# Two 3x3 convolutions of a Trainium2 kernel as 64x32 instead of 32x32 products, with shifted strips copied inside SBUF

## What is computed

```python
x = x + _L0_conv_ref(_gn(x), w_real, w_imag, b_real, b_imag)  # rfftn, complex 3x3 conv, irfftn
x = x + _L1_conv_ref(_gn(x))                                  # gates per row of one channel against another
x = x + _L2_conv_ref(_gn(x), L2_conv_W)                       # 3x3 convolution, 16 -> 16 channels, padding 1
x = x + _L3_conv_ref(_gn(x), L3_conv_weight)                  # the same, other weights
```

## Time and profile before

| | |
|---|---|
| runs | 4795.12, 4809.72, 4811.2 us, median 4809.72 |
| profiled execution | span 4801.7 us from its first to its last instruction; no time of its own beside the span is recorded, the median lies 8.0 us above it |
| busy | PE 95%, PEld 61%, DVE 61%, ACT 52%, POOL 0% |
| mean granted TensorE clock | 0.968 of full speed |
| DMA | 468 MB, 97 GB/s over the span |

### The profile page before, as it was taken

The page is one execution under the profiler, slowest core; times in us unless marked ns, Lnnn a source line. Parts: engine busy times, 40 slices in busy tenths (PEclk is TensorE's granted clock), DMA queues, the critical chain, the costliest instruction groups (busy, mean ns, idle before and its releaser), DMA issues.

```text
span 4801.7 us, 221653 instructions
## 1 busy us (share of the span) xinstructions
PE 4548.2 (95%) x84784; PEld 2936.4 (61%) x84784; DVE 2925.9 (61%) x10604; ACT 2487.6 (52%) x7085; POOL 3.2 (0%) x14
## 2 busy tenths in 40 slices
PE   4999999999999999999999999999999999998889
PEld 1555675556655566556665556655666557655566
DVE  1777717766277662777527765377744777257770
ACT  4455355544555445554455544555445554544435
POOL 0000000000000000000000000000000000000000
PEclk8999999999999899999999989999899999999999
DMA  7443015630166202662036510366004650034304
GB/s 196 111 124 100 4 29 172 176 102 4 47 177 176 79 3 61 178 177 63 4 86 177 176 41 3 105 176 174 24 3 120 177 163 19 3 111 122 90 4 143
DMA packets 290069, 468.11 MB, mean 97 GB/s; under 512 B 25392, under 2 KB 92144, under 8 KB 289264
## 3 DMA queue, kind: packets, MB, share of 16 engines
q1 hardware_dynamic: 289392, 458.29, 33.1%
HBM read 323.98 MB, written 134.22 MB: 95 GB/s over the span
## 4 chain that ended last, share of the span: by engine, by line
PE 91%; DVE 3%; issue 3%; DMA 1%; SPq 1%; ACT 1%; ACTq 0%; DVEq 0%
PE ps L1247 35%; PE ps L1165 19%; PE ps L1150 18%; PE ps L1158 6%; PE ps L1174 5%; PE ps L1024 5%; DMA x<-x 1%; PE ps L1273 1%; PE ps L1070 1%; PE ps L1071 0%; PE ps L1097 0%; PE ps L1305 0%; PE ps L1219 0%; SPq L360 0%; PE ps L1112 0%
## 5 line engine op out<-in xcount | busy, mean ns | idle before, releaser
L1247 PE MATMUL ps<-x,conv_s 32*32 32x512 f32 x49104 | 1728.0, 603 | 20.8 <-DVE x L948 16.7
L1247 PEld LDWEIGHTS ps<-x,conv_s 32*32 32x32 f32 x49104 | 1252.8, 103 | 437.9 <-issue 196.1
L563 ACT ACTIVATE x<-ps,vec 128x256 f32 (+1 forms) x1024 | 492.0, 495 | 1003.1 <-PE ps L1165 1003.1
L1165 PE MATMUL ps<-hil,shared 128*128 128x256 f32 x4096 | 993.6, 386 | 0.0
L814 DVE COPY vsb<-ps 128x512 f32<-128x512 f32 x512 | 329.9, 686 | 1043.6 <-PE ps L1150 1043.6
L1165 PEld LDWEIGHTS ps<-hil,shared 128*128 128x128 f32 x4096 | 740.2, 190 | 273.8 <-issue 194.1
L802 DVE SCALAR_TENSOR_TENSOR shared<-xin,trig 128x256 f32<-128x256 f32 x2048 | 821.6, 441 | 57.3
L629 ACT ACTIVATE x<-ps,vec 64x512 f32<-64x512 f32 (+1 forms) x768 | 527.2, 686 | 395.9 <-PE ps L1247 385.6
L1150 PE MATMUL ps<-shared 32*32 32x512 f32 x16384 | 656.4, 605 | 0.0
L620 ACT ACTIVATE x<-ps,vec 128x512 f32 x512 | 347.9, 685 | 439.6 <-PE ps L1247 439.6
L1150 PEld LDWEIGHTS ps<-shared 32*32 32x32 f32 x16384 | 306.2, 104 | 280.0 <-issue 216.8
(11 more groups left out here) (170 smaller groups left out, 2720.6 us busy)
## 6 DMA issues: line engine op xcount, KB each, us to landing
xin<-x SPq DMA_DIRECT2D x512, 256.0 KB
out<-x SPq DMA_DIRECT2D x512, 256.0 KB
shared<-x SPq DMA_DIRECT2D x448, 256.0 KB, 5.0
shared<-t_strip SPq DMA_DIRECT2D x512, 96.0 KB, 3.6
x<-x SPq DMA_DIRECT2D x64, 256.0 KB, 8.1
x<-t_proj SPq DMA_DIRECT2D x1, 2048.0 KB, 11.8
hil<-t_hil SPq DMA_DIRECT2D x1, 560.0 KB, 12.1
trig<-t_trig SPq DMA_DIRECT2D x1, 512.0 KB, 11.8
```

Of the source, the lines that this page charges most:

```text
L563: ins = nc.scalar.activation(split_in(strip_of(s))[:, q, :], split_in(ps[:, bank, :])[:, q, :], ACT.Identity, bias=v1(MEAN), accum_out=sum ...
L1165: mm = pe.matmul(split_in(ps[:, BY + 2 * odd + e, :])[:, int(q < 2), :], xt[:, e, q, :], hil[:, q, 0:HALF], start=False, stop=True, skip_g ...
L1247: mm = pe.matmul(ps[TM * cg:TM * cg + TM, banks[k], :], conv_s[TM * rg:TM * rg + TM, kw, second, :], x1[TM * rg:TM * rg + TM, of, kw:kw + ...
```

## The change

- **64x32 products.** Each output quarter is now made by one product per tap, with 64 partitions of input (two quarters, half the array's rows) and 64x32 weights: 8 products a tap and pair, 24 a pair instead of 48, on 8 tiles of 64x32. `halved`, LAG2 and LAG3 go. The order over a pair is tile by tile with the two strips in turn; each of the 8 tiles is used once per tap. `conv_s` keeps its size; its 64-row blocks have two kinds.
- **Shifted strips.** The two quarters that an output needs lie in one half of the partitions for half of the outputs only. For the others a second copy of the strips, with the quarters moved, is kept in `ring`: up to 12 strips in layer 2 (3 groups of 2 pairs, RING2) and 8 in layer 3 (2 groups, RING3). It is filled by DMA from `x1` (SBUF to SBUF). Layer 2: per group of two pairs 6 DMAs on SP, two of 32 partitions x 4 strips and four of 32 x 2; the first two pairs apart, three of their DMAs each on SP and three on ScalarE's queue, after `keep_zh`. Layer 3: 2 DMAs per group, 96 x 4 strips and 32 x 4. Either way 1 MiB a group. A group's copy waits for gates (layer 2), for the last eviction of layer 2 (layer 3), and for the group that last used its slots: three groups back in layer 2, two groups back in layer 3.
- **Squares** of layer 2: ScalarE squares the even strip of a pair after evicting it, VectorE the odd one; `red` and its copy go. GATES_AHEAD is 16, before it was 12.
- **Memory.** `ring` lies over `planes`, `wst` and part of `strip`, so the first `make_planes` of the next image waits until all but two pairs of layer 3 are done, those of strips 2 and 3 until all are, and four table loads move to after group 2 of layer 3.
- Stores of the last image go out two groups behind in layer 3. The bias of layer 3 takes 12 products (24 records), before 24 (L1305, 48 records). The pads of `ring` are set by one more operation on POOL and one on DVE.

```diff
-DEPTH2, LAG2 = 4, TAPS + 1
-DEPTH3, LAG3 = 3, TAPS
+DEPTH2, DEPTH3 = 4, 3
+BLOCKS = 4
+RING2, RING3 = 3, 2
+COPIES2, COPIES3 = 6, 2
+CONV_FREE = 3
...
-GATES_AHEAD = 3 * GROUP
+GATES_AHEAD = 4 * GROUP
...
+            def copy2(i):
+
+                for n in range(2):
+                    sp.wait_ge(gated, i * STRIPS + 2 * n + 3)
+                    sp.sem_inc(s_sp, 1)
+                    for to, of in blocks2(PAIRS - 1 - n, 1, slot2(n))[0::2]:
+                        sp.dma_start(to, of).then_inc((copied0, copied2[0])[n], 16)
+                for g in range(1, PAIRS // 2):
+                    sp.wait_ge(gated, i * STRIPS + min(STRIPS, BLOCKS * g + BLOCKS + 1))
...
+                        sp.wait_ge(convolved, cv(i, 1 + 2 * (g - RING2) + 2))
...
+                    for to, of in blocks2(PAIRS - 2 - 2 * g, 2, slot2(2 * g + 1)):
+                        sp.dma_start(to, of).then_inc(copied2[g % RING2], 16)
+
+            def copy3(i, g):
+
+                if g == 0:
+                    sp.wait_ge(evicted, ev(i, 1 + STRIPS))
+                    sp.sem_inc(s_sp, 1)
+                if g >= RING3:
+                    sp.wait_ge(convolved, cv(i, 1 + PAIRS + 2 * (g - RING3) + 2))
...
+                sp.dma_start(ring[0:P - TM, slot:slot + BLOCKS, 1:1 + N], x1[TM:P, s:s + BLOCKS, 1:1 + N]).then_inc(copied3[g % RING3], 16)
+                sp.dma_start(ring[q3, slot:slot + BLOCKS, 1:1 + N], x1[q0, s + 1:s + 1 + BLOCKS, 1:1 + N]).then_inc(copied3[g % RING3], 16)
...
-                act.wait_ge(convolved, i * CONVOLVED + 1)
+                for n in range(2):
+                    act.wait_ge(gated, i * STRIPS + 2 * n + 3)
+                    act.sem_inc(s_act, 1)
+                    for to, of in blocks2(PAIRS - 1 - n, 1, slot2(n))[1::2]:
+                        act.dma_start(to, of).then_inc((copied0, copied2[0])[n], 16)
+                act.wait_ge(convolved, cv(i, 1))
...
+                    nc.scalar.activation(junk, strip_of(STRIPS - 2 - n * 2), ACT.Square,
+                                         accum_out=cols[:, 3, bass.ds(STRIPS - 2 - n * 2, 1)]).then_inc(a_c_squared, 1)
...
+                dve.wait_ge(convolved, cv(i, -2))
+                dve.sem_inc(s_dve, 1)
                 for k in range(2):
                     make_planes(steps_of(k), k, k, u0 + 1, 0)
+                dve.wait_ge(convolved, cv(i, 0))
...
+                def products(banks, outputs, strips, kw):
+
+                    for j in range(TILES):
+                        for k in range(2):
+                            cg, h, slot, kind = outputs(strips[k])[j]
+                            rows = slice(HP * h, HP * h + HP)
+                            of = x1[rows, strips[k], kw:kw + N] if slot is None else ring[rows, slot, kw:kw + N]
+                            mm = pe.matmul(ps[TM * cg:TM * cg + TM, banks[k], :], conv_s[rows, kw, kind, :], of,
+                                           start=(kw == 0), stop=(kw == TAPS - 1), skip_group_check=True)
+                    return mm
```

More of the change, by code:

```diff
@@ L53 @@
 AXB, AXC, AXS = 0, 1, 2
+CONV_BLOCKS = ((0, 0, 0), (1, 0, 1), (2, 0, 0), (3, 0, 1), (1, 1, 0), (3, 1, 1))
 ZR = 96
@@ L112, in tables @@
     eye_conv = np.zeros((P, 2, TAPS, 2, TM))
-    for rg in range(TILES):
+    for rg, kind, second in CONV_BLOCKS:
         for c in range(C):
-            eye_conv[TM * rg + C + c, :, 1, 0, c] = 1.0
-            eye_conv[TM * rg + c, :, 1, 1, C + c] = 1.0
+            if second:
+                eye_conv[TM * rg + c, :, 1, kind, C + c] = 1.0
+            else:
+                eye_conv[TM * rg + C + c, :, 1, kind, c] = 1.0
     zsel = np.zeros((ZR, P + ZR))
@@ L162, in placed @@
         for kw in range(TAPS):
-            for second in range(2):
+            for rg, kind, second in CONV_BLOCKS:
                 for r in range(2):
@@ L350, in ev, with cv, slot2, blocks2 @@
             return i * EVICTED + n + EVICT_FREE
+        def cv(i, n):
+            return i * CONVOLVED + n + CONV_FREE
+        q0, q1, q2, q3 = (slice(TM * k, TM * k + TM) for k in range(TILES))
+        def slot2(n):
+            return BLOCKS * (n // 2 % RING2) + 2 * (1 - n % 2)
+        def blocks2(first, pairs, slot):
+            low = first * 2
+            across = lambda of, s, to: (ring[to, slot:slot + 2 * pairs, 1:1 + N], x1[of, s:s + 2 * pairs, 1:1 + N])
+            second = lambda of, s, to, k: (ring[to, slot + k:slot + 2 * pairs:2, 1:1 + N], x1[of, s:s + 2 * pairs:2, 1:1 + N])
+            above = across(q1, low - 1, q2) if low else (ring[q2, slot + 1:slot + 2 * pairs, 1:1 + N], x1[q1, 0:2 * pairs - 1, 1:1 + N])
+            return (above, across(q3, low, q0), second(q0, low, q3, 0), second(q2, low, q3, 1), second(q2, low + 1, q1, 0), second(q0, low + 1, q1, 1))
         @block.sync
@@ L442, in image @@
                     for pair in range(2):
-                        load_pair(i + 1, pair, 2 * pair)
-                for n in range(PAIRS):
-                    if more and n >= PAIRS - (STRIPS - DEFERRED):
-                        sp.wait_ge(evicted, ev(i, 1 + STRIPS + 2 * n + 2))
-                        sp.sem_inc(s_sp, 1)
-                        store(i, n - (PAIRS - (STRIPS - DEFERRED)))
-                    elif not more:
-                        for e in range(2):
-                            store(i, 2 * n + e)
+                        for e in range(2):
+                            load_x(i + 1, pair * 2 + e, pair, 2 * pair + e)
+                copy2(i)
+                for g in range(PAIRS // 2):
+                    copy3(i, g)
+                    if more and g == RING3:
+                        for pair in range(2):
+                            load_tables(i + 1, pair, 2 * pair)
+                    for e in range(BLOCKS if not more else 2):
+                        if not more and g >= RING3:
+                            store(i, BLOCKS * (g - RING3) + e)
+                        elif more and g >= PAIRS // 2 - (STRIPS - DEFERRED) // 2:
+                            store(i, 2 * (g - PAIRS // 2 + (STRIPS - DEFERRED) // 2) + e)
+                if not more:
+                    for s in range(STRIPS - BLOCKS * RING3, STRIPS):
+                        store(i, s)
             image(0, True, False)
```

165 lines of the change are left out of this document (83 added, 82 removed).

## The result

Before, the runs gave a median of 4810.5 us (4795.1 to 4811.7, 4 runs), after it 4670.8 us (4660.4 to 4680.2, 4 runs): a ratio of 0.9714, 95% interval 0.9690 to 0.9737. The change makes the kernel 139.6 us faster. The forecast was 4525, a gain of 286. The median lies inside the forecast's range of 4455 to 4720, but only about half of the gain came (49%).

What follows compares the result with a forecast made beforehand. TensorE bounds the kernel, by something in feeding 16 tiles. Gains of 138 (layer 2), 133 (layer 3), 8 (last image), 9 (bias), less 2, make 286 us: 4801.7 to 4516 span, 4524 with 8 added; forecast 4525, range 4455 to 4720.

Steps and rivals of the forecast that it cites:

- Part 1, the streaming: Layer 2's products: rounds of 0.43 us on 8 tiles, a pair 2.56 us instead of 3.10, gaining 16.2 us an image.
- rival 2: Streaming in layers 2 and 3 gains nothing, as the loss belongs to four tiles per row group; 4795 us, chance 0.1.
- Part 2, the start: Start of layer 2: 4 us lost waiting for first copies, 5 us gained by the second pair, net +1 an image.
- Part 3, layer 3: Layer 3 falls from 120.2 to 99.1 us; 19 us taken as gained in each of seven images, 133 in all.
- T: Time of a group's copies in layer 3, 6.0 us; what exceeds one group of 5.12 us is waited for.
- the term of 2.4 us: Part of the layer 3 copies' time that isn't data: fastest 256 KB landing of 3.3 us, of which 0.9 is data.
- that base: Layer 3 with no copy ever waited for: 95.6 us, from stream, slow start and column work.
- Rival 1: Copies over 32 or 96 partitions run slower than loads: 4565 us at 4.8 us per MiB, 4685 at 5.8; 4600-4780, chance 0.2.
- The last image: Its layer 3: copies plus stores, 7.2 us a group, leave 109.8 us as it is, 90 at full overlap; 8 us taken.
- Small parts: Bias halved gains 8.6 us in all, sharing squares 0 after the last pair, late `make_planes` loses 2.
- If both squares had stayed on DVE: Layer 2: DVE's work of 2.7 us would have capped each pair, against 2.06 with one square moved to ACT.
- Rival 3: Copies at half the loads' rate, 146 GB/s, 7.2 us per MiB, make the kernel slower: 4945 us, chance 0.08.

Runs made afterwards that it cites:

- 5: Also wide3: changed kernel, layer 3's copies from the second group on over 128 partitions x 2 strips, straight, same bytes; 4636.0 us.
- 6: Also straight3: changed kernel, layer 3's copies from the second group on keep 96 and 32 partitions but stay in their own rows; 4689.5 us.
- 3: Also nostore: changed kernel with 56 of the last image's 64 stores left out, copies kept; 4618.3 us.
- 4: Changed kernel with the last image's layer 3 copies of 32 partitions issued on ScalarE's queue, stores staying on SP's; 4690.1 us.
- 2: Changed kernel with layer 3's copies made pair by pair, in half as large pieces and four slots of two strips; 4605.3 us.
- 10: Also dvesq: changed kernel with both squares of layer 2 on VectorE again; 4675.8 us.
- twoact: Changed kernel with the 32-partition copy issued on ScalarE's queue from layer 3's third group on, beside SP's of 96; 4699.4 us.

## Why the prediction was half right

**Part 1, the streaming: right.** 2.575 us a pair instead of 2.56, and the weight loads (timeline, start of layer 3) come 8 at a time, 0.43 us apart:

```profile
1705.86 0.12 PEld L1332 LDWEIGHTS ps<-x,conv_s 64*32 64x32 f32 x4 [0.30 <-issue]
1705.87 0.12 PEld L1332 LDWEIGHTS ps<-shared,conv_s 64*32 64x32 f32 x4
...
1706.29 0.12 PEld L1332 LDWEIGHTS ps<-x,conv_s 64*32 64x32 f32 x4 [0.30 <-issue]
```

Four tiles share each half of the rows and a round still takes 1024 columns at 2.4 GHz, so rival 2 fell. The loads of both halves come while products of both halves are in flight, and nothing of the 0.43 us is lost to them. The Trainium skill, "TensorE: Matmul & The Clock Gate", Part 3, says that weight loads overlap products only when the row group differs; this trace does not agree with it. What costs 16 tiles 0.09 us a round is still open: no run took it apart.

**Part 2, the start: right in the loss, and in the gain by luck.** The start of layer 2, third image (gate, first copies, tail product):

```profile
1596.29 0.74 DVE L1035 TENSOR_SCALAR x<-x,cols,gate_b  x2 [0.24 <-issue]
...
1598.94 4.41 SPq L447 DMA_DIRECT2D shared<-x  x6
1598.94 4.13 ACTq L690 DMA_DIRECT2D shared<-x  x6
...
1603.65 1.03 PE L1357 MATMUL ps<-x,conv_s 64*32 64x512 f32 x1 [5.67 <-DMA shared<-x]
```

TensorE starts 7.4 us after the first gate, against 3.2 in the earlier trace rows: 4.1 us later, forecast 4. The second pair is evicted 10.9 us after the start instead of the 13.4 forecast. The bias takes 0.88 us instead of 2.16. Layer 2 with the bias was forecast at 138 + 8.6 us and brought 143.6. Two errors cancel in that. The third image, from which the 19.2 us before were read, is not typical: its first 10 us of layer 2 ran at a granted clock of 0.50, and so two others, while in five images the second pair was evicted 13.1 to 14.8 us after the start. The mean is 16.0 before and 10.3 after, so the gain was 5.6 us a start, against 5 forecast. No copy of layer 2 was late, at a DMA share of 0.78 (forecast 0.7).

**Part 3, layer 3: this is the step that failed.** Its value for the copies' time, T = 2.4 + 3.6 = 6.0 us, was too small, and so were the 3.5 us of waiting that followed from it; and it put what the clock loses after a wait at nothing. The landing of L469 (768 KB) and, on the lines of the copies, L470's median of 6.8 us:

```profile
L469 SPq DMA_DIRECT2D shared<-x x128: 615/626/1962, 567.2 to 4640.1; - x128
...
DMA to landing us min/median/max: 5.6/6.2/9.6
```

L470 is issued 0.67 us after L469, so T is 6.8 + 0.67 = 7.5 us. Of the 1.5 us that were missing, 0.6 are the rate: the earlier trace rows gave 293 GB/s from DMAs over 128 partitions, and experiments 5 and 6 show some 248 for DMAs over 96 and 32. The other 0.9 are in the term of 2.4 us for all that isn't data: it came from the fastest landing of the earlier trace rows, 3.3 us. With the median of the same row, 5.0, the prediction had 7.7 as its upper bound, close to what was measured. To it comes the way to TensorE. The queue of SP, third image:

```profile
1707.95 0.62 SPq L469 DMA_DIRECT2D shared<-x  x1
...
1713.56 0.64 SPq L469 DMA_DIRECT2D shared<-x  x1
```

From the issue at 1707.95 to the product at 1716.07 are 8.1 us, and two pairs give 5.15 of cover: a wait of some 3 us (the row shows 3.15) instead of 0.9.

In the trace of this image six of the fourteen later groups have a pause, 12.3 us in all, and the column work or the pause before hides the others; stepping the model of the forecast with 8.1 us in place of 6.0 gives 12.4 (an estimate). After one of the pauses, at 1772.94, a pair took 3.9 us from its first to its last start instead of 2.2, at a lower granted clock: 1.7 us more. That is nearly all of the 14.8 us that copies cost in this image, where 3.5 were forecast.

The other 3.2 us: without copies the layer takes 98.8 us, not 95.6; that base was summed too low, by some 1.2 us between the last pair and the next image's first product, which waits for ScalarE, 0.7 at the slow start, 0.7 of column work and 0.5 of streaming. Together 14.5 us, from 99.1 to 113.6. Over seven images 38 us came, where I took 19 each, 133: 95 of the 151 us that are missing by the profiled spans.

The form of the model, a wait of T less one group, held. Rival 1 had the figure (T of 7 to 8 us), but its mechanism, a lower rate over few partitions, is only 0.6 of the 1.5 us; its 103.9 us was 10 too low for the reasons given. That its total range of 4600 to 4780 holds the result is luck: it got there through a slower layer 2, which did not come, and without the loss in the last image.

The Trainium skill, "SBUF — State Buffer", Door 1, says that a DMA over 32 or 64 partitions reaches 8 of 16 DMA ports, some 218 GB/s. Experiments 5 and 6 agree with it in kind; the 248 GB/s measured are 14% above its figure, and three quarters of these bytes go over 96 partitions, for which it has none.

**The last image: the second failed step.** "2 MiB at 293 GB/s are 7.2 us a group, which leaves the 109.8 as it is" took throughput alone as the limit. A group took 9.3 to 10.3 us in the middle of it: copies were issued at 4525.68, 4535.00, 4544.70 and 4555.04:

```profile
4525.68 1.17 SPq L469 DMA_DIRECT2D shared<-x  x1
4526.89 2.30 SPq L470 DMA_DIRECT2D shared<-x  x1
4529.37 5.50 SPq L439 DMA_DIRECT2D out<-x  x4
4535.00 1.21 SPq L469 DMA_DIRECT2D shared<-x  x1
```

That is 2 MiB at 203 to 225 GB/s, with the engines 72% busy. The copies land later after their issue (the 256 KB one after 8.9 us, against 6.7 without stores), and TensorE pauses before nearly every group, 14 times, 47 us in all. After 11 of the pauses it begins again at the lower level of its clock. The timeline of PE after one of them:

```profile
4544.52 1.08 PE L1332 MATMUL ps<-x,conv_s 64*32 64x512 f32 x4 [4.39 <-DMA shared<-x]
...
4545.33 1.12 PE L1332 MATMUL ps<-x,conv_s 64*32 64x512 f32 x4
...
4546.18 1.12 PE L1332 MATMUL ps<-x,conv_s 64*32 64x512 f32 x4
...
4548.36 0.62 PE L1332 MATMUL ps<-x,conv_s 64*32 64x512 f32 x4
4548.79 0.62 PE L1332 MATMUL ps<-x,conv_s 64*32 64x512 f32 x4
```

Rounds are 0.85 us apart, then 0.43. These pairs took 3.5 to 4.3 us from first to last start instead of 2.2, together 19 us, for which the prediction had no term. So of the 70 us that copies cost here 47 are pauses and most of the rest is the clock; with copies and no stores (3) it was 18 us of pauses and no slow pair. 8 us gained became 46 lost, 54 more of the 151 us. That it is the stores beside the copies in the engines, and not only in the queue, is shown (3, 4); why the engines are idle for a quarter of the time is not, and neither narrower nor wider copies helped (2, 5).

**Small parts.** "If both squares had stayed on DVE, its 2.7 would have capped the pair at 2.7" is wrong (10): I took the mean busy time of one where the distance from start to start counts. That `make_planes` costs 2 us can't be seen beside the rest. Rival 3 needed copies at 166 GB/s or less; in layer 2 the window shows 187 GB/s moved, and no product there waited for a copy after the first.

## What to carry to other kernels

When a transfer is started by the freeing of its own buffer, count from the last product on the old data to the first on the new: issue, latency, data and the wake-up, and compare that with the work that the other buffers hold; more and smaller slots in the same bytes were worth 65 us here. Take the median time to landing, not the fastest, and add what the clock loses after a pause: here it was 19 us beside 47 us of pauses. Take a DMA's rate only from DMAs over as many partitions. Where a stage has stores beside it that others don't have, cost it by itself, and keep the old form there if it needs no transfers.

## What the runs showed of the hardware

- SBUF-to-SBUF copies, in slices with busy engines: 363 to 385 GB/s with 128 partitions in a DMA (wide3), 199 to 309 with 96 and 32 (mean 248 in the changed kernel), whether rows change quarter or not (straight3), and from one queue or two (twoact).
- Copies of 1 MiB and stores of 1 MiB together got 197 GB/s at a share of 0.72. In the last image copies without stores cost 21 us over stores without copies (85.4 us), both together 70.
- After a pause of the products of some microseconds the granted clock was often at its lower level for most of a pair: after 11 of 14 pauses in the last image of the changed kernel, 1.3 to 2.1 us each; after none of 13 in nostore, whose pauses are shorter (18 us in all).
- 8 tiles of 64x32 stream float32 at 0.43 us a round of 8 records with weight loads hidden; 16 tiles of 32x32 need 0.52 for a round of 16.
- A float32 square of 128x512 on VectorE lasts 0.68 us in the profile, and the next starts 0.61 us after it (dvesq).
